# Attention with routed experts in one kernel: the reciprocal product moved between two turns, the expert slot reordered, keys copied between exponentials

## The chip, the cores and the metric

One NeuronCore of one Trainium2 chip runs the whole program. The metric is device time in microseconds (us). A core has five engines that run side by side and meet at semaphores: TensorE (PE, with its weight loads shown as PEld), VectorE (DVE), ScalarE (ACT), GpSimd (POOL) and SyncE (SP), which here only issues DMAs. Each engine takes its own instructions in the order in which the program lists them, so the place of a waiting instruction in that order is what this case is about.

## The reference, cut to what matters

```python
xn = layernorm(x)                                  # x: 16 x 512 tokens of 128
h  = rmsnorm(xn) * norm_scale
q, k, v = h @ wq * 64**-0.5, h @ wk, h @ wv        # 16 heads of 64
attn = softmax(q @ k.T) @ v @ w_out + b_out        # within each of the 16 blocks of 512
logits = silu(xn @ rw1 + rb1) @ rw2 + rb2          # router, 8 experts, the best 2
ffn = sum over the two experts e of prob_e * (silu(xn @ w1[e] + b1[e]) @ w2[e] + b2[e])
out = x + attn + ffn
```

All in float32. The experts' hidden width is 512.

## The kernel before, in words

**Ticks and units.** Each of the NB = 16 blocks of 512 tokens has 32 pieces of attention work, which are done in "ticks". There are TIMES = 256 ticks G; four of them make a unit u = G // 4 (64 units), and k = G % 4 is the tick's place in its unit. A unit is 4 head pairs (GH) by half of a block's queries; it has eight steps, two for each tick. A step s of unit u is: scores on PE (L313, into the PSUM banks 0 to 3, two at a time), the row maxima on DVE (`maxima`, L555), two exponentials on ACT with their row sums (`probs`, L911), and a turn (32x32 transposes) on DVE (`turn_probs`, L563). When all eight turns of unit u-1 are done, PE multiplies them by the values in the ticks k = 0 and k = 1 of unit u (`weighted`, L332, 128 matmuls in each), into the banks 4 to 7. DVE's `weighted` (L572, two instructions) multiplies that by the reciprocals of the row sums, which is what frees the four banks; PE's `project_out` (L345, "OP") follows in tick k = 2, and DVE adds its result into `acc` (L595 or L598).

**The reciprocals' way.** `denominators` (L581, L585) makes and turns the reciprocals at the start of tick k = 0; SP writes them to a DRAM scratch with four DMAs (`spread`, L1239), waits for these, and reads them back, spread over the partitions, as RB with two DMAs (L1244). DVE's `weighted` waits for RB.

**Keys, queries, values of the next unit.** In tick k = 2 PE makes the next unit's queries (L298, two banks), in tick k = 3 two of the next group's key tiles (L283 to L286) and two of its value tiles (L271). ACT copies them out (L890, L884, L918). The two key tiles of a tick with G % 8 = 7 are needed by the scores of the very next tick.

**The banks 4 to 7 are a ring** (`Ring`): each user takes the next bank in the order in which PE's program lists them, and waits until the bank's last user was read (`came_free`). At k = 2 the ring is aligned to bank 4.

**The second half.** Router and scatter run in the ticks below 128. From tick 139 on, the 39 expert tiles of 512 rows (NT = 39) are worked in `SLOTS`: ten at 139, 151, ... 247 (k = 3) and 29 at k = 2 of the units 35 to 63. In the slot of tile i the kernel turns the rows of tile i+1 on PE ("turn", L239 into `xg`), does the second product of tile i-1 ("y", 32 matmuls L472 into `w2`) and the first product of tile i ("h", four chunks of three matmuls, L222 to L224). ACT has, for "turn", one copy (L983) and, for each chunk of "h", a tanh (L995) and a copy with bias (L997), which frees the chunk's bank. DVE has, for "turn", the low half (L800), for "y" two instructions (`give_back`, L813 and L817), and for each chunk one `halves` (L806), which needs the chunk's L995 and L997. `LATE` puts the last two `halves` of a slot into the next tick, behind that tick's two maxima. SP fetches weights and rows at "h" of chunk 0; POOL adds the rows to the output at "back".

**Order.** `PLAN[G]` is the order written out by hand for the experts; all engines follow it. A tick's other work comes ahead of it on PE and ACT, and on DVE it stands behind the tick's turns and `project_out`. What the next tick's maxima wait for on DVE is therefore everything of the slot that DVE has in this tick.

Of the kernel before, what the change touches and what calls it, by code (L numbers as in the profile page):

```python
# [25 lines left out]
NC = HID // P  # L26
# [53 lines left out]
def block_kernel(nc, x, wq, wk, wv, wout, ns, bout, rw1, rb1, rw2, rb2, w1, w2, bias, brows, ident, tri, consts, out):  # L80
    T = x.shape[0]
    NB = T // S
# [7 lines left out]
    with ExitStack() as ctx:  # L90
# [100 lines left out]

        SLOTS = sorted([FIRST + 12 * k for k in range(NT - (UNITS - FIRST // 4 - 1))] + [4 * u + 2 for u in range(FIRST // 4 + 1, UNITS)])
        PLAN = {G: [] for G in range(TIMES + 8)}
        LATE = {G: [] for G in range(TIMES + 8)}
        PLAN[FIRST - 1].append((0, "turn"))
        for i, G in enumerate(SLOTS):
            if i + 1 < NT:
                PLAN[G].append((i + 1, "turn"))
            if i:
                PLAN[G].append((i - 1, "y"))  # L200
            PLAN[G] += [(i, "h", c) for c in range(NC)]
            LATE[G + 1] += [(i, c) for c in (2, 3)]
            if i:
                PLAN[G].append((i - 1, "back"))
        PLAN[TIMES - 1].append((NT - 1, "y"))
        PLAN[TIMES].append((NT - 1, "back"))

# [306 lines left out]
        def _(eng):  # L514
# [42 lines left out]
            def turn_probs(g, s):  # L557
                step = STEPS * g + s
                slot = place_of(g, s)[0]
                dve.wait_ge(sem["act_exp"], 2 * step + 2)  # L560
                if step >= RING:
                    dve.wait_ge(sem["pe_PV"], (step - RING) // STEPS + 1)
                dve.do.transpose(PT[:].rearrange("p c k q -> p (c k) q")[:, :, 32 * slot:32 * slot + 32],  # L563
                                 PR[:, step % PRB].rearrange("p r k -> p (r k)")).then_inc(sem["dve_tr"])
# [121 lines left out]
            def counts(r):  # L686
                dve.wait_ge(sem["dve_gate"], 15 * r + 13)
                for t in range(QT):
                    if t or r:
                        dve.wait_ge(sem["dve_pm"], 5 * r + t)  # L690
                    else:
                        dve.wait_ge(sem["dve_pm0"], 1)
                    if r >= 2:
                        dve.wait_ge(sem["pe_pos"], r - 1)
                    dve.do.tensor_tensor(PM[:, r % 2, t + 1], PM[:, r % 2, t], mask[:, t], ALU.add).then_inc(sem["dve_pm"])
                dve.wait_ge(sem["dve_pm"], 5 * r + QT)
                dve.wait_ge(sem["pe_pos"], r)
                dve.do.tensor_copy(PM[:, 1 - r % 2, 0], PM[:, r % 2, QT]).then_inc(sem["dve_pm"])
# [103 lines left out]
            def halves(i, c):  # L802
                n = i * NC + c
                dve.wait_ge(sem["act_zt"], n + 1)
                dve.wait_ge(sem["act_zz"], n + 1)
                dve.do.scalar_tensor_tensor(HH[:, i % 2, c], ZT[:, n % 2], 1.0, HH[:, i % 2, c], ALU.add, ALU.mult).then_inc(sem["dve_s"])  # L806
# [13 lines left out]
            def experts(G):  # L820
                if G == EARLY * GB + 3:
                    totals()
                for i, what, *c in PLAN[G]:
                    if what == "turn":
                        rows_low(i)
                    if what == "y":
                        give_back(i)
                    if what == "h" and c[0] < 2:
                        halves(i, c[0])

            dve.do.memset(junk[:], 0.5).then_inc(sem["dve_junk"])
# [10 lines left out]
            for G in range(TIMES + 8):  # L842
                u, k = divmod(G, 4)
                if k == 0 and 0 < u < UNITS:
                    denominators(u - 1)
                if k == 2 and 0 < u <= UNITS:
                    weighted(u - 1)
                if u < UNITS:
                    maxima(u, 2 * k)
                    maxima(u, 2 * k + 1)  # L850
                attending(G)
                between(G)
                for i, c in LATE[G]:
                    halves(i, c)
                if u < UNITS:
                    turn_probs(u, 2 * k)
                    if G % 8 == 2 and 0 < G // 8 <= NB:
                        counts(G // 8 - 1)
                    turn_probs(u, 2 * k + 1)
                route(G)  # L860
                if k == 2 and 0 < u <= UNITS:
                    project_out(u - 1)
                if G == TIMES - 1:
                    denominators(u)
                experts(G)

        @block.scalar
        def _(eng):
# [26 lines left out]
                act.do.copy(XT[:], bank[BANK["xT", r]]).then_inc(sem["act_xTs"])  # L895

            def alone(G):
                return G >= 8 * NB and G % 8 == 7 and G not in SLOTS

            def probs(g, s):  # L900
                step = STEPS * g + s
# [24 lines left out]
            def attending(G):  # L926
                b, h = divmod(G, GB)
                u, k = divmod(G, 4)
                g, first = u // 2 + 1, u % 2 * 2
                if k == 3 and g < 2 * NB:  # L930
                    if G >= 8 * NB and not alone(G):
                        keys(g, first)
                    if not alone(G):
                        keys(g, first + 1)
                    values(g, first)
                    values(g, first + 1)
                if G < 2:
                    values(0, 2 * G)
                    values(0, 2 * G + 1)
# [512 lines left out]
```

## Time and profile before

| | before |
|---|---|
| median of 3 runs | 1888.17 us (1884.29 to 1891.51) |
| the profiled execution | 1887.85 us, its span 1886.0 us |
| mean granted TensorE clock | 0.997 |
| ticks 0 to 127, a pair of units | 52.5 us |
| ticks 140 to 255, three units (with three slots at k = 2 and one at k = 3) | 96.5 us |

The page counts an engine as busy while an instruction of it runs. Matmuls are pipelined and overlap, so PE's share says little; how long a tick lasts is read from DVE's first maxima of a tick (L555) to that of the next, and its cause from the chain of waits and the timeline.

### The profile page before, as it was taken

To read this page: it belongs to the slowest core of one execution; us is meant where nothing else is said; L and a number is where in the kernel's file an instruction comes from. 1 tells how busy PE (TensorE), PEld (TensorE's weight loads), DVE (VectorE), ACT (ScalarE), POOL (GpSimd) and SP (SyncE) were. 2 spreads that over 40 slices of the span, in tenths; PEclk is the share of its full clock that TensorE was granted. 3 is DMA by queue.
4 is the path that set the end of the run, shared out by engine and by line. 5 is a ranking of instruction groups with operands and counts; after the bars stand their busy time and mean duration, and the time that the engine had idled before them with its cause. 6 is when DMAs were issued, how large, how long until landed. Compare 5 with 4: busy or idle time off the path is not lost.

```text
span 1886.0 us, 74660 instructions
## 1 busy us (share of the span) xinstructions
PE 1817.7 (96%) x32554; PEld 1177.0 (62%) x32554; DVE 1625.3 (86%) x2297; ACT 1209.1 (64%) x2987; POOL 733.0 (39%) x641
## 2 busy tenths in 40 slices
PE   8999999999999999998999999999999999999997
PEld 5555555555555555554567766767676667666765
DVE  6999999999999999989888888788888888888886
ACT  6666776666666666664666675666676666666663
POOL 4244655444544445432023334324324333333143
PEclk9999999999999999999999999999999999999999
DMA  3033321111111111111433434333433333333333
GB/s 96 22 83 109 101 95 52 42 48 37 48 37 48 48 48 46 30 40 56 110 74 78 90 73 90 78 84 78 89 74 66 92 65 87 76 84 78 79 74 56
DMA packets 154487, 130.15 MB, mean 69 GB/s; under 512 B 27664, under 2 KB 139024, under 8 KB 154128
## 3 DMA queue, kind: packets, MB, share of 16 engines
q1 hardware_dynamic: 123568, 104.65, 20.3%
q0 software_dynamic: 30592, 20.73, 8.1%
q8 instruction: 255, 4.18, 0.9%
q14 instruction: 72, 0.59, 0.1%
HBM read 93.15 MB, written 34.27 MB: 68 GB/s over the span
## 4 chain that ended last, share of the span: by engine, by line
PE 40%; ACT 28%; DVE 18%; issue 12%; DMA 1%; POOL 0%; POOLq 0%; SPq 0%; ACTq 0%; DVEq 0%
ACT PR L911 18%; PE pair L332 11%; DVE NM L555 8%; PE pair L472 8%; PE pair L313 7%; DVE PT L563 4%; PE pair L345 3%; ACT ZT L995 3%; ACT HH L997 3%; PE pair L298 3%; DVE OT L572 3%; ACT KS L884 1%; PE pair L239 1%; PE pair L388 1%; PE pair L271 1%
## 5 line engine op out<-in xcount | busy, mean ns | idle before, releaser
L911 ACT ACTIVATE PR<-pair,NM 128x512 f32<-128x512 f32 x1024 | 696.3, 697 | 536.9 <-DVE NM L555 536.4
L563 DVE STREAM_TRANSPOSE PT<-PR 128x1024 f32<-128x1024 f32 x512 | 633.2, 1241 | 119.2 <-ACT PR L911 105.7
L555 DVE TENSOR_REDUCE NM<-pair 128x2 f32<-128x1024 f32 x512 | 598.0, 1208 | 19.6 <-PE pair L313 18.9
L313 PE MATMUL pair<-KS,QS 64*32 64x512 f32 x8192 | 505.3, 598 | 16.6 <-ACT PR L911 9.3
L332 PE MATMUL pair<-PT,V 32*64 32x256 f32 x16384 | 479.7, 378 | 17.9 <-ACT HH L997 9.7
L332 PEld LDWEIGHTS pair<-PT,V 32*64 32x64 f32 x16384 | 383.6, 131 | 166.6 <-issue 107.3
L1174 POOL DMA_INDIRECT out<-YS,IDW x156 | 248.4, 1592 | 536.8 <-DVE YS L817 334.3
L313 PEld LDWEIGHTS pair<-KS,QS 64*32 64x32 f32 x8192 | 122.7, 106 | 261.7 <-issue 157.4
L911 ACT ACTIVATION_READ_ACCUMULATOR PR<-pair,NM 128x1 f32 x1024 | 218.9, 214 | 0.0
L995 ACT ACTIVATE ZT<-pair,BT 128x512 f32<-128x512 f32 x156 | 109.8, 704 | 108.1 <-PE pair L224 108.0
L1132 POOL DMA_INDIRECT slots<-XR,IDX x128 | 124.4, 972 | 73.9 <-issue 38.5
L472 PE MATMUL pair<-E,HH 128*128 128x128 f32 x1248 | 148.1, 277 | 2.9 <-DVE HH L806 2.9
L472 PEld LDWEIGHTS pair<-E,HH 128*128 128x128 f32 x1248 | 144.1, 194 | 4.4 <-DVE HH L806 3.8
L806 DVE SCALAR_TENSOR_TENSOR HH<-ZT,HH 128x512 f32<-128x512 f32 x156 | 104.1, 688 | 43.6 <-ACT HH L997 43.6
L298 PE MATMUL pair<-HF,WQ 128*128 128x256 f32 x512 | 126.1, 389 | 10.1 <-DVE OT L572 9.3
L298 PEld LDWEIGHTS pair<-HF,WQ 128*128 128x128 f32 x512 | 92.1, 190 | 62.2 <-DVE OT L572 49.5
L1121 POOL TENSOR_TENSOR TH<-TH,HS 128x512 f32<-128x512 f32 x64 | 82.1, 1282 | 120.1 <-ACT HS L951 120.1
L345 PE MATMUL pair<-OT,WO 128*128 128x256 f32 x512 | 123.6, 384 | 2.2 <-DVE OT L572 2.2
L271 PE MATMUL pair<-WV,HF 128*32 128x128 f32 x4096 | 125.1, 274 | 0.0
L271 PEld LDWEIGHTS pair<-WV,HF 128*32 128x32 f32 x4096 | 107.8, 110 | 23.4 <-issue 23.3
L345 PEld LDWEIGHTS pair<-OT,WO 128*128 128x128 f32 x512 | 94.7, 190 | 37.7 <-issue 9.5
L997 ACT ACTIVATE HH<-pair,BT 128x512 f32<-128x512 f32 x156 | 110.4, 708 | 0.0
(129 smaller groups left out, 1798.1 us busy)
## 6 DMA issues: line engine op xcount, KB each, us to landing
RB<-l_rows SPq DMA_DIRECT2D x128, 256.0 KB, 4.3
E<-w_tab SPq DMA_DIRECT2D x39, 512.0 KB
XG<-slots SPq DMA_DIRECT2D x39, 264.0 KB, 4.0
E<-in_w SPq DMA_DIRECT2D x39, 256.0 KB, 3.9
xin<-in_x SPq DMA_DIRECT2D x16, 256.0 KB, 2.8
XQ<-in_x SPq DMA_DIRECT2D x16, 256.0 KB, 3.1
l_rows<-RT SPq DMA_DIRECT2D x256, 2.0 KB
w_tab<-SPL SPq DMA_DIRECT2D x8, 512.0 KB, 2.6
```

Source lines behind the costliest of these rows:

```text
L271: m = pe.do.matmul(bank[bk][32 * a:32 * a + 32, j * P:j * P + P], HF[:, keys], WV[:, pair], start=True, stop=True, tile_position=(0, 32 * a))
L298: m = pe.do.matmul(bank[bk][:, 256 * i:256 * i + 256], WQ[:, pair], HF[:, 256 * half:256 * half + 256], start=True, stop=True)
L313: m = pe.do.matmul(bank[2 * (s % 2) + r][32 * c:32 * c + 32, :], QS[rows, u % 2, c, at:at + 32], KS[rows, g % 2, c, :], start=True, stop=T ...
L332: m = pe.do.matmul(bank[GH + a][DH * c:DH * c + DH, 0:256], V4[rows, g % 2, k, DH * c:DH * c + DH], moving, start=(k == 0), stop=(k == 15) ...
L345: m = pe.do.matmul(bank[bk][:, 0:256], WO[:, GH * (u // 2 % 2) + a, :], OT[:, a, :], start=(a == 0), stop=(a == GH - 1))
L472: m = pe.do.matmul(bank[bk][:, t * P:(t + 1) * P], HH[:, i % 2, c, t * P:(t + 1) * P], E2[:, i % 2, c * P:(c + 1) * P], start=(c == 0), st ...
L555: dve.do.tensor_reduce(NM[:, step % 4], pairs[s % 2][:], AX.X, ALU.max, negate=True).then_inc(sem["dve_max"])
L563: dve.do.transpose(PT[:].rearrange("p c k q -> p (c k) q")[:, :, 32 * slot:32 * slot + 32], PR[:, step % PRB].rearrange("p r k -> p (r k)" ...
L911: act.do.activation(PR[:, step % PRB, r, :], bank[2 * (s % 2) + r], ACT.Exp, bias=NM[:, step % 4, r:r + 1], accum_out=RS[:, g % 2, r, at:a ...
L995: act.do.activation(ZT[:, n % 2], ps, ACT.Tanh, bias=BT[:, i % 3, 8 + c:9 + c], scale=0.5).then_inc(sem["act_zt"])
L997: act.do.activation(HH[:, i % 2, c], ps, ACT.Identity, bias=BT[:, i % 3, c:c + 1]).then_inc(sem["act_zz"])
L1174: pool.do.indirect_dma_start(out, bass.IndirectOffsetOnAxis(ap=IDW[:, i % 4, t, 0:1].bitcast(U32), axis=0), YS[:, i % 2, t, :], None, comp ...
```

## The change

Three edits. (1) DVE's `weighted(u-1)` moves from the head of tick k = 2, ahead of the maxima, to tick k = 1, between its two turns. (2) In `PLAN` the four chunks "h" of a slot come first, then "turn", then "y"; all four `halves` are in the slot's own tick, and `LATE` is gone. (3) `alone(G)` now holds in the first half too: in the ticks with G % 8 = 7 below 128 ACT copies both key tiles between the exponentials of the tick's two steps, instead of one between and one behind. In the second half it stays as it was.

```diff
         PLAN = {G: [] for G in range(TIMES + 8)}
-        LATE = {G: [] for G in range(TIMES + 8)}
         PLAN[FIRST - 1].append((0, "turn"))
         for i, G in enumerate(SLOTS):
+            PLAN[G] += [(i, "h", c) for c in range(NC)]
             if i + 1 < NT:
                 PLAN[G].append((i + 1, "turn"))
             if i:
-                PLAN[G].append((i - 1, "y"))
-            PLAN[G] += [(i, "h", c) for c in range(NC)]
-            LATE[G + 1] += [(i, c) for c in (2, 3)]
-            if i:
-                PLAN[G].append((i - 1, "back"))
+                PLAN[G] += [(i - 1, "y"), (i - 1, "back")]
...
-                    if what == "h" and c[0] < 2:
+                    if what == "h":
                         halves(i, c[0])
...
-                if k == 2 and 0 < u <= UNITS:
+                if k == 2 and u == UNITS:
                     weighted(u - 1)
...
-                for i, c in LATE[G]:
-                    halves(i, c)
                 if u < UNITS:
                     turn_probs(u, 2 * k)
                     if G % 8 == 2 and 0 < G // 8 <= NB:
                         counts(G // 8 - 1)
+                    if k == 1 and u:
+                        weighted(u - 1)
                     turn_probs(u, 2 * k + 1)
...
             def alone(G):
-                return G >= 8 * NB and G % 8 == 7 and G not in SLOTS
+                return G % 8 == 7 and G not in SLOTS
...
-                    if G >= 8 * NB and not alone(G):
+                    if G in SLOTS or G % 8 == 3 and G >= 8 * NB:
                         keys(g, first)
```

## Rows read from the trace of the kernel before

**Rows 1.** The page: busy us, share of the span, instructions.

```profile
PE 1817.7 (96%) x32554; PEld 1177.0 (62%) x32554; DVE 1625.3 (86%) x2297; ACT 1209.1 (64%) x2987; POOL 733.0 (39%) x641
```

**Rows 2.** Who waited for whom, whole span: us in total, times, longest.

```profile
ACT PR L911 <- DVE NM L555: 536.4, 214, 6.1
ACT ZT L995 <- PE pair L224: 108.0, 38, 3.7
```

**Rows 3.** Timeline, slot at k = 2: start, duration, engine, line, [idle before].

```profile
1590.67 2.34 DVE L555 TENSOR_REDUCE NM<-pair 128x2 f32<-128x1024 f32 x2
...
1592.17 1.89 PE L345 MATMUL pair<-OT,WO 128*128 128x256 f32 x8
...
1594.33 3.74 PE L472 MATMUL pair<-E,HH 128*128 128x128 f32 x32
...
1595.70 1.25 DVE L563 STREAM_TRANSPOSE PT<-PR 128x1024 f32<-128x1024 f32 x1 [1.07 <-ACT PR L911]
...
1596.87 0.39 DVE L598 TENSOR_TENSOR acc<-pair,acc 128x256 f32<-128x256 f32 x1
...
1598.11 0.69 DVE L813 SCALAR_TENSOR_TENSOR YS<-pair,B 128x512 f32<-128x512 f32 x1 [0.25 <-PE pair L472]
...
1598.80 0.69 ACT L995 ACTIVATE ZT<-pair,BT 128x512 f32<-128x512 f32 x1 [2.65 <-PE pair L224]
1598.83 0.69 DVE L817 TENSOR_TENSOR YS<-YS,IDW 128x512 f32<-128x512 f32 x1
...
1599.96 0.69 ACT L995 ACTIVATE ZT<-pair,BT 128x512 f32<-128x512 f32 x1
```

**Rows 4.** Timeline, DVE alone: that slot's end, then the slot at k = 3.

```profile
1601.97 2.36 DVE L555 TENSOR_REDUCE NM<-pair 128x2 f32<-128x1024 f32 x2
...
1605.45 2.37 DVE L563 STREAM_TRANSPOSE PT<-PR 128x1024 f32<-128x1024 f32 x2
...
1611.17 0.69 DVE L813 SCALAR_TENSOR_TENSOR YS<-pair,B 128x512 f32<-128x512 f32 x1 [1.80 <-PE pair L472]
...
1615.42 1.18 DVE L555 TENSOR_REDUCE NM<-pair 128x2 f32<-128x1024 f32 x1
```

**Rows 5.** Timeline, ACT alone, the slot at k = 3.

```profile
1606.97 1.18 ACT L918 COPY V<-pair 128x512 f32<-128x512 f32 x2
```

**Rows 6.** Timeline, DVE alone, the slot at k = 2 two units on.

```profile
1657.17 2.34 DVE L555 TENSOR_REDUCE NM<-pair 128x2 f32<-128x1024 f32 x2
...
1668.78 2.36 DVE L555 TENSOR_REDUCE NM<-pair 128x2 f32<-128x1024 f32 x2
```

**Rows 7.** Timeline, DVE alone, first half: an even unit's tick k = 1.

```profile
388.93 2.58 DVE L563 STREAM_TRANSPOSE PT<-PR 128x1024 f32<-128x1024 f32 x2
```

**Rows 8.** Timeline, DVE alone, first half: an odd unit's ticks k = 1 and k = 3.

```profile
413.38 2.36 DVE L555 TENSOR_REDUCE NM<-pair 128x2 f32<-128x1024 f32 x2 [0.53 <-PE pair L313]
...
416.12 2.59 DVE L563 STREAM_TRANSPOSE PT<-PR 128x1024 f32<-128x1024 f32 x2
...
430.87 1.25 DVE L563 STREAM_TRANSPOSE PT<-PR 128x1024 f32<-128x1024 f32 x1 [0.58 <-ACT PR L911]
```

**Rows 9.** Timeline, PE and ACT, first half: second half of the weighted values, the second key copy.

```profile
386.14 3.71 PE L332 MATMUL pair<-PT,V 32*64 32x256 f32 x128
...
414.06 3.71 PE L332 MATMUL pair<-PT,V 32*64 32x256 f32 x128
...
430.71 0.60 ACT L884 COPY KS<-pair 128x512 f32<-128x512 f32 x1
```

**Rows 10.** Timeline, SP's reads of RB in two units, and DVE's product in the first.

```profile
1164.64 1.25 SPq L1244 DMA_DIRECT2D RB<-l_rows  x2
...
1171.42 1.29 DVE L572 TENSOR_TENSOR OT<-pair,RB 128x512 f32<-128x512 f32 x2 [0.71 <-DMA RB<-l_rows]
...
1581.93 1.25 SPq L1244 DMA_DIRECT2D RB<-l_rows  x2
```

**Rows 11.** All reads of RB (L1244): time from issue to landing.

```profile
DMA to landing us min/median/max: 3.5/4.3/5.7
```

## The prediction

> **What bounds the kernel now.** I read the page first, then the waits, then the timeline of all engines over one repetition in each half. The page [rows 1] names no bound: PE has always something in flight, DVE is busy for 86%, ACT for 64%. The waits [rows 2] show where to look: ACT waits 536 us for maxima from DVE and, in 38 of the 39 expert slots, 108 us in all for the first product on PE. The second of these is what edit 2 takes up. But an idle ACT costs nothing unless ACT is what ends last, so each edit has to be followed to the next maxima.
>
> In the timeline the bound changes hands within each unit. In the first half, PE is late from an even unit's tick k = 2 to the maxima of the next odd unit's tick k = 1, which wait 0.53 us for its scores [rows 8]; from there on DVE, with ACT's exponentials between its maxima and its turns, is late until the next even unit's tick k = 2. In a k = 2 slot, PE's row of work (output projection, turn, second product, first product) ends with ACT's first tanh, and ACT's four chunks then end last [rows 3].
>
> **Edit 2, slots at k = 2.** Let T be the start of the tick's first maxima, 1590.67 in rows 3; the next tick's stand at T+11.30 in rows 4. A later slot has 1668.78-1657.17 = 11.61 [rows 6]. I take 11.45, their middle, for each of the 28 such slots ahead of the last.
>
> After the change PE starts the first product at the projection's end, T+3.4 (1592.17+1.89) [rows 3], and ACT can begin its tanh when the last exponential is done, some 4.9 after T (the turn that waits for it starts at 1595.70, T+5.0 [rows 3]; the copy L983 that stands there now comes last). So ACT's wait of 2.65 [rows 3] is gone. What is late next follows from two orders.
>
> First the ring. A k = 2 tick takes its banks from bank 4 on: queries, (a turn of h or of acc in half of the blocks' ticks,) the projection OP, and then the slot's. The fourth chunk of "h" is now always four places behind OP and so gets its bank; it must wait for DVE's sum into acc. Before, the second product or a turn stood between, and the fourth chunk came long after. The sum ends at 1596.87+0.39 = T+6.6, behind the turn that waits 1.07 for the exponentials, at which nothing is changed [rows 3]. PE then has, one after the other: three matmuls 0.70 (rows 3: the first tanh at 1598.80 follows the second product's end and one such chunk), turn 0.43, second product 3.74 [rows 3]. That ends at T+6.65+0.70+0.43+3.74 = T+11.5.
>
> Second DVE's order. The two `give_back` now stand behind all four `halves` and ahead of the next maxima. Start to start they take 0.72 (1598.83-1598.11) and the second 0.69 [rows 3]: T+11.55+0.72+0.69 = T+12.95 for the next maxima. ACT's side is earlier: chunks of 1.16 (1599.96-1598.80) [rows 3] from T+4.9 end at T+9.5, its copy at T+10.2, the last `halves` at T+10.3, the low half at T+10.9.
> So the tick grows from 11.45 to 12.95, **+1.5; 28 slots: +42 us**. With no wait for the sum the second product would end 0.6 earlier, and this would be +0.9, or +25.
>
> **What gives some of it back.** In the tick behind a slot the two late `halves` are gone and the four turns and maxima run as in a tick without slot.
> - Slot at k = 3 (10). Before 1615.42-1601.97 = 13.45 [rows 4], and the following ticks k = 0 and 1 12.6 together, as in a timeline of the next unit. After, from the first maxima M: exponentials until M+3.95, four copies of keys and values at M+6.0 (1606.97 and 1.18 are the last two of them) [rows 5], and only then the four chunks, whose banks these copies free: chunk 1 free at M+8.2, second product until M+12.0, the two give-backs, reciprocals 0.4: M+13.8, +0.35. Then 5.2 and 6.55 for the two ticks, with the product waiting 0.3 for PE: -0.85. Together **-5 us** for ten.
> - Plain k = 3 tick behind a slot, G % 8 = 3 (10): -0.5, but the copies of the values end later against DVE, so the weighted values of the next unit begin 0.35 later and edit 1 waits for them: -0.5+0.5, **0 us**.
> - G % 8 = 7, not in a slot (9): -0.2 and, in edit 1, -0.2: **-3 us**.
> - The last unit and the tail: the last slot +2, all `halves` earlier, so the last second product no longer waits: **-1 us**.
>
> **Edit 1 in the first half.** The work only changes place on DVE; what changes is what it waits for. In even units the turn ends at 388.93+1.25 = 390.2, PE's weighted values at 386.14+3.71 = 389.85 [rows 7, 9]: no wait, and the 0.1 between the two turns is covered; -0.18 for 15 units, -2.7. In odd units the turn ends at 416.12+1.25 = 417.4 but PE at 414.06+3.71 = 417.8 [rows 8, 9]: the product starts there, 0.36 later than the second turn did: 15 units (two with 0.7), +6.1. PE itself gains a little where its queries had waited for the product, but it then waits for ACT's queries as before: nothing.
>
> The product now is 1.2 us earlier (one turn) and so nearer to RB's landing. SP issues the reads between 2.8 (1581.93, a unit begun at 1579.08) and 4.4 (1164.64, one begun at 1160.21) after the unit's first maxima, in others up to 4.9, and the second is landed some 5.2 after the first's issue (0.6 to 0.9 for its own issue, 4.3 median) [rows 10, 11]. DVE is ready at 9.15 (even) or 10.2 (odd units of the first half). With 5.2 on every unit's issue, ten of the fifteen even first-half units wait 0.1 to 0.85, in sum +6.8 (with the covered 0.1), and the second half +5.5. Bounds: 0, if all land as the earliest, at 7.5; 63 x 1.4 = +88, if all land as the latest, 11.2 in rows 10, where the product waited even in its old place. I take **+12 us**, since 5.2 is the middle of what the landings show.
> The Trainium skill (DMA: Bandwidth & Descriptors, section "Anatomy of one DMA — SWDGE (gpsimd) path") gives a DMA about 2.0 us fixed plus its bytes by 436 GB/s; as an estimate from that page, write and read back would be done some 5 to 6 after the maxima and the product would never wait, which takes these 12 us off. The landings of rows 11, 3.5 at the least, speak against it here.
>
> **Edit 3.** In the 16 ticks with G % 8 = 7 of the first half the second key copy (0.60, 0.58 start to start) [rows 9] goes ahead of the second step's exponentials, whose turn on DVE already waits 0.58 for them [rows 8]. DVE has nothing else to do there and is late from there to the next unit's k = 2. PE's scores, which now wait for the copy, come earlier, but the maxima behind them are held by DVE. **16 x 0.58 = +9.3 us.** Bounds 0 (if PE's earlier scores paid it back) and 9.3; DVE's rows from 430.87 on run without a gap, so I take the upper.
>
> **Sum** on the profiled execution: 42-5-3-1 (slots), -2.7+6.1+9.3 (first half), +12 (RB) = +57.7; 1887.85+57.7 = **1945 us**. That execution is within 0.4 us of the median, so no correction.
>
> **Rivals.**
> - *ACT was the bound of the slots (faster).* If the next maxima could be made while ACT does its chunks, all of the 108 us [rows 2] would go: 1887.85-108+24 = about 1805. It decides at one point: whether the second product ends before T+9. For it: the chain of before passes through PE's second product and ACT's chunks in every slot. Against: three chunks, OP's bank and the turn stand ahead of the second product now, and it alone takes 3.74. Chance 0.05.
> - *The sum isn't waited for long, and the second key copy costs nothing (slower by less).* The slots +25 in place of +42, edit 3 nothing: 1945-17-9 = 1919. Against: bank and order are fixed in the program. Chance 0.13.
> - *RB is late every time (slower by more).* Half way to the bound of +88: 1945+38 = 1983. For it: latencies of L1244 up to 5.7 and issues of up to 4.9. Chance 0.06.
> - *Nothing to be seen*: gains in the ticks behind the slots equal the losses. It would take 1.5 us more gain behind each slot than the late `halves` (1.3 us of DVE) can give. Chance 0.03.
> - *Forecast*: 1945, own range 1928 to 1964, chance 0.73.
>
> **Numbers.** The range takes in the forecast's and reaches to the smaller loss: 1920 to 1968. About 0.5% (9 us) is what a measurement of this kernel can tell from no change. Faster 0.05, same 0.03, slower 0.92.
>
> **What would show each step.** In the profile after: first maxima to first maxima of a k = 2 slot 12.9 (before 11.3 to 11.6), PE idle about 1 us ahead of the fourth chunk until acc, and DVE's L813 counterpart waiting for the second product; ACT's wait for the first product from 108 to under 20 us, its wait for maxima larger by about as much. In the first half: the product waiting for PE in odd units, for RB in some even ones; a wait of 1.15 in place of 0.58 ahead of the last turn of the G % 8 = 7 ticks. A k = 2 slot of under 12.3 would make the bank's step wrong; one under 11.4 the whole forecast.

## The result, and the profile after

The changed kernel took 1962.12 us (median of four runs, 1958.83 to 1963.69), the kernel before 1889.25 us beside it: ratio 1.0387, with a 95% interval of 1.0362 to 1.0413, so slower. The profiled execution took 1962.82 us, its span is 1961.0 us, 75.0 more than before, at a mean granted clock of 0.994. The prediction said 1945 us with a range of 1920 to 1968: sign and mechanism came out, the size was 17 us short.

The page of the kernel after (busy us, share of the span, instructions), to be laid beside rows 1:

```profile
PE 1838.1 (94%) x32554; PEld 1180.0 (60%) x32554; DVE 1640.9 (84%) x2297; ACT 1210.3 (62%) x2987; POOL 734.4 (37%) x641
```

The work on DVE and ACT is what it was, within 1%, and its shares fell: nearly all of the 75 us are idle time. Where they stand is told by the waits. The waits of the kernel after, whole span (who waited for whom, us in total, times, longest), to be laid beside rows 2. The edit moved every line number: L551 here was L555, L907 was L911, L568 was L572, L309, L328 and L468 were L313, L332 and L472.

```profile
ACT PR L907 <- DVE NM L551: 715.9, 253, 6.1
...
PE pair L218 <- DVE acc L594: 23.9, 15, 2.2
...
DVE OT L568 <- PE pair L328: 22.6, 30, 8.4
...
PE pair L218 <- DVE acc L591: 16.2, 14, 1.5
...
DVE OT L568 <- DMA RB<-l_rows: 15.6, 21, 1.9
```

ACT's 108.0 us for the first product [rows 2] are gone, and its wait for the maxima grew by 179.5 us: ACT now waits in one place for longer than it did in two. Three waits are new or have grown. PE's matmul of the first product (L218) waits for DVE's sum into acc in 29 slots, 40 us in all. DVE's product waits for PE in 30 units where it did in one, the last, and for RB in 21 units where it did in one (rows 10).

The slot itself. Timeline of the kernel after, all engines, a slot at k = 2 (start, duration, engine, line, [idle before]); rows 3 and 4 show the same of before:

```profile
1685.80 2.31 DVE L551 TENSOR_REDUCE NM<-pair 128x2 f32<-128x1024 f32 x2
...
1690.64 0.72 ACT L991 ACTIVATE ZT<-pair,BT 128x512 f32<-128x512 f32 x1
...
1690.82 1.25 DVE L559 STREAM_TRANSPOSE PT<-PR 128x1024 f32<-128x1024 f32 x1 [1.07 <-ACT PR L907]
...
1691.98 0.39 DVE L594 TENSOR_TENSOR acc<-pair,acc 128x256 f32<-128x256 f32 x1
...
1692.43 0.50 PE L218 MATMUL pair<-X,E 128*128 128x512 f32 x1 [0.96 <-DVE acc L594]
...
1693.66 3.74 PE L468 MATMUL pair<-E,HH 128*128 128x128 f32 x32
...
1697.44 0.69 DVE L809 SCALAR_TENSOR_TENSOR YS<-pair,B 128x512 f32<-128x512 f32 x1 [0.56 <-PE pair L468]
1698.16 0.69 DVE L813 TENSOR_TENSOR YS<-YS,IDW 128x512 f32<-128x512 f32 x1
1698.77 2.35 DVE L551 TENSOR_REDUCE NM<-pair 128x2 f32<-128x1024 f32 x2
```

Maxima to maxima: 1698.77-1685.80 = 12.97, against 11.30 and 11.61 before [rows 3, 4, 6]; the prediction said 12.95. Read from the end: the maxima follow the second give-back without a gap, the first give-back waited 0.56 for the second product, this one stands behind the fourth chunk of the first product, and that waited 0.96 for the sum, which stands behind the turn that waits 1.07 for the exponentials. (0.96 is the shortest of these waits; the 29 have 1.38 in the mean and 2.23 at most. Their start varies, their end is the sum's.) ACT starts its first tanh at T+4.84, where rows 3 have T+8.13, and nothing is gained by these 3.3 us.

The first half. Timeline of the kernel after, DVE alone, an odd unit's tick k = 1 (first two rows) and k = 3; rows 8 show the same of before:

```profile
426.52 1.25 DVE L559 STREAM_TRANSPOSE PT<-PR 128x1024 f32<-128x1024 f32 x1
...
428.27 1.29 DVE L568 TENSOR_TENSOR OT<-pair,RB 128x512 f32<-128x512 f32 x2 [0.51 <-PE pair L328]
...
442.16 1.25 DVE L559 STREAM_TRANSPOSE PT<-PR 128x1024 f32<-128x1024 f32 x1 [1.07 <-ACT PR L907]
```

The product stands between the turns and waits 0.51 for PE; the last turn of the G % 8 = 7 tick waits 1.07 in place of 0.58. Both were to be seen by the prediction, at 0.36 and at 1.15.

**The ledger.** First maxima to first maxima of every tick, after less before, on the two profiled executions:

| where | predicted | measured | ticks, after and before |
|---|---|---|---|
| 28 slots at k = 2 | +42 | +43.5 | mean 13.08 and 11.5 |
| 10 slots at k = 3 and the two ticks behind | -5 | +1.3 | 14.05 and 13.44 typical |
| plain G % 8 = 3 ticks and the two behind | 0 | +4.0 | -5.2, +1.8, +7.4 |
| G % 8 = 7 outside slots and the two behind | -3 | +0.4 | -1.8, 0, +2.2 |
| the product's waits for RB, second half | +5.5 | in the three rows above | 10.3 in 12 waits |
| last slot and tail | -1 | +4.1 | slot 13.17 and 9.60, tail +0.6 |
| first half, odd units, k = 1 | +6.1 | +7.9 | 6.86 and 6.42 typical |
| first half, even units, k = 1, with RB's waits | +4.1 | +7.7 | 6.19 to 8.51 |
| first half, keys | +9.3 | +7.6 | 7.81 and 7.32 |
| everything else before tick 136 | 0 | -1.6 | |
| sum | 58 | 75 | |

### The profile page after: what moved, and what is told of

Its sections match the earlier page's. It is cut to its first block, busy times and chain, and to the rows that moved or that the text cites. A ratio compares the mean times of both kernels' runs of the same rounds, so it can differ in the third digit from the quotient of the medians.

```text
span 1961.0 us, 74661 instructions
## 1 busy us (share of the span) xinstructions
PE 1838.1 (94%) x32554; PEld 1180.0 (60%) x32554; DVE 1640.9 (84%) x2297; ACT 1210.3 (62%) x2987; POOL 734.4 (37%) x641
## 4 chain that ended last, share of the span: by engine, by line
PE 32%; DVE 24%; ACT 22%; issue 9%; DMA 9%; SPq 2%; POOL 0%; POOLq 0%; ACTq 0%; DVEq 0%
ACT PR L907 14%; PE pair L328 13%; DVE NM L551 8%; PE pair L468 7%; DVE PT L559 7%; PE pair L309 6%; DMA RB<-l_rows 5%; DVE OT L568 4%; DMA l_rows<-RT 3%; ACT QS L886 3%; ACT KS L880 2%; SPq L1235 2%; PE pair L384 1%; ACT ZT L991 1%; DVE YS L809 1%
## 5 line engine op out<-in xcount | busy, mean ns | idle before, releaser
L907 ACT ACTIVATE PR<-pair,NM 128x512 f32<-128x512 f32 x1024 | 694.3, 690 | 716.1 <-DVE NM L551 715.9
L551 DVE TENSOR_REDUCE NM<-pair 128x2 f32<-128x1024 f32 x512 | 596.3, 1205 | 15.2 <-PE pair L309 14.0
L309 PE MATMUL pair<-KS,QS 64*32 64x512 f32 x8192 | 511.7, 600 | 21.0 <-ACT PR L907 18.3
L328 PE MATMUL pair<-PT,V 32*64 32x256 f32 x16384 | 479.0, 379 | 14.6 <-ACT XT L891 3.1
L328 PEld LDWEIGHTS pair<-PT,V 32*64 32x64 f32 x16384 | 386.7, 132 | 160.7 <-issue 85.9
L309 PEld LDWEIGHTS pair<-KS,QS 64*32 64x32 f32 x8192 | 119.7, 106 | 265.2 <-ACT PR L907 130.8
L907 ACT ACTIVATION_READ_ACCUMULATOR PR<-pair,NM 128x1 f32 x1024 | 211.4, 206 | 0.0
L802 DVE SCALAR_TENSOR_TENSOR HH<-ZT,HH 128x512 f32<-128x512 f32 x156 | 111.8, 718 | 69.8 <-ACT HH L993 68.8
L468 PE MATMUL pair<-E,HH 128*128 128x128 f32 x1248 | 149.7, 279 | 2.9 <-ACT HH L993 2.9
L468 PEld LDWEIGHTS pair<-E,HH 128*128 128x128 f32 x1248 | 145.5, 195 | 6.3 <-DVE HH L802 3.7
L218 PE MATMUL pair<-X,E 128*128 128x512 f32 x156 | 70.2, 450 | 51.4 <-DVE acc L594 23.9
```

Of the source, the lines that this page charges most:

```text
L309: m = pe.do.matmul(bank[2 * (s % 2) + r][32 * c:32 * c + 32, :], QS[rows, u % 2, c, at:at + 32], KS[rows, g % 2, c, :], start=True, stop=T ...
L328: m = pe.do.matmul(bank[GH + a][DH * c:DH * c + DH, 0:256], V4[rows, g % 2, k, DH * c:DH * c + DH], moving, start=(k == 0), stop=(k == 15) ...
L468: m = pe.do.matmul(bank[bk][:, t * P:(t + 1) * P], HH[:, i % 2, c, t * P:(t + 1) * P], E2[:, i % 2, c * P:(c + 1) * P], start=(c == 0), st ...
L551: dve.do.tensor_reduce(NM[:, step % 4], pairs[s % 2][:], AX.X, ALU.max, negate=True).then_inc(sem["dve_max"])
L907: act.do.activation(PR[:, step % PRB, r, :], bank[2 * (s % 2) + r], ACT.Exp, bias=NM[:, step % 4, r:r + 1], accum_out=RS[:, g % 2, r, at:a ...
```

## The experiments

The kernels ran in three groups, each on a chip of its own. In the second group the kernel before took 1888.09 us, as at first; in the first it took 2042.39 and in the third 2029.53. A ratio is therefore read only against the runs of its own group; what the traces show of the first and third group's chips comes with the first experiments. "Ticks" are always first maxima to first maxima.

### Each edit alone (first and third group)

e1_product and e1_again make edit 1 alone:

```diff
-                if k == 2 and 0 < u <= UNITS:
+                if k == 2 and u == UNITS:
                     weighted(u - 1)
...
+                    if k == 1 and u:
+                        weighted(u - 1)
                     turn_probs(u, 2 * k + 1)
```

e2_slot and e2_again make edit 2 alone:

```diff
+            PLAN[G] += [(i, "h", c) for c in range(NC)]
             if i + 1 < NT:
                 PLAN[G].append((i + 1, "turn"))
...
-            PLAN[G] += [(i, "h", c) for c in range(NC)]
-            LATE[G + 1] += [(i, c) for c in (2, 3)]
...
-                    if what == "h" and c[0] < 2:
+                    if what == "h":
                         halves(i, c[0])
```

e3_keys and e3_again make edit 3 alone:

```diff
-                return G >= 8 * NB and G % 8 == 7 and G not in SLOTS
+                return G % 8 == 7 and G not in SLOTS
...
-                    if G >= 8 * NB and not alone(G):
+                    if G in SLOTS or G % 8 == 3 and G >= 8 * NB:
                         keys(g, first)
```

e1_product:

> Edit 1 alone on the kernel before: the product with the reciprocals moved between the turns of tick k = 1, the slots and the key copies as before. Theory (the parts add up, and each is a wait on DVE): +20 to +26 us over before (ratio 1.011 to 1.014); odd units' tick k = 1 of the first half 6.86 in place of 6.42 us (the product waits for PE's weighted values), even ones 6.2 where RB is in time and up to 7.6 where it is late. Rival (RB is late only because the reordered slots move the weights' and rows' transfers onto it): within 6 us of before, even units of the first half 6.2 throughout.

e1_again:

> Edit 1 alone on the kernel before, once more, on whichever chip comes. Theory, from the ticks of the runs so far: on a chip without the late instructions +13 to +20 us (ratio 1.007 to 1.011), nearly all of it in the first half, since the old order's slots are bound by PE and take back in tick k = 2 what tick k = 1 loses; the slots at k = 2 about 0.4 shorter. Rival (edit 1 costs the same in both halves): +25 to +33 us.

e2_slot:

> Edit 2 alone on the kernel before: the slot's chunks first, then the turn, then the second product, all four halves in the slot's tick. Theory: the k = 2 slots last 12.95 us in place of 11.5, the k = 3 slots 0.6 more, their following tick 1.0 less, plain k = 3 ticks 0.2 to 0.5 less: +35 to +43 us over before (ratio 1.019 to 1.023). Rival (the slots' order costs only together with the moved product, whose later maxima push the sum into acc back): under +20 us.

e2_again:

> Edit 2 alone on the kernel before, once more. Theory: +33 to +42 us (ratio 1.0175 to 1.022), all of it from tick 139 on; edits 1 and 2 together then cost 10 to 15 us more than their sum, because the slots no longer take back what the product's waits cost. Rival (the parts add up): +52 us, what is left of after's 77 when 17 and 8 are taken off.

e3_keys:

> Edit 3 alone on the kernel before: both key copies between the exponentials in the ticks with G % 8 = 7 below 128. Theory: each such tick 0.5 us longer (7.8 for 7.3), because DVE's last turn waits for exponentials that stand behind one more copy: +7 to +9 us (ratio 1.004 to 1.005). Rival (PE's scores, released 0.5 us earlier by the copy, pay it back): 0, the following tick k = 0 shorter by 0.5.

e3_again:

> Edit 3 alone on the kernel before, once more. Theory: 0.45 to 0.5 us in each of the 16 ticks with G % 8 = 7 below 128, +7 to +8 us (ratio 1.0035 to 1.0045) on a chip without the late instructions; there, as in the first group, nothing. Rival (PE's earlier scores pay it back): within 2 us of before on every chip.

| edit alone | first group | third group |
|---|---|---|
| 1, the product | 2053.13, ratio 1.0045 [1.0029, 1.006] | 2043.99, 1.0073 [1.0057, 1.0088] |
| 2, the slot | 2077.34, 1.0173 [1.0157, 1.0189] | 2065.45, 1.0169 [1.0153, 1.0184] |
| 3, the keys | 2043.27, 1.0006 [0.9995, 1.0017] | 2035.19, 1.0024 [1.0015, 1.0034] |

Edit 2 carries most of the loss, +35 and +36 us. Its slots at k = 2 have 13.00 us in both, as in the whole change. Edit 1 adds 11 and 14 us, edit 3 adds 1 (its interval takes in 0) and 6 (its interval does not). Of the forecasts, e1_product's (+20 to +26) and e3_keys' (+7 to +9) were missed, and e3_again's, that nothing would be seen on such a chip. In sum these are 47 and 56 us, where the first chip showed 73 for the whole; so either the parts don't add, or these chips hide some of it. The first question went to the second group; on the second the trace of e3_again has something to say. Timeline of e3_again, PE alone, then DVE alone ("<-issue": the engine waited for nothing that the profile shows), in one tick with G % 8 = 7 of the first half:

```profile
483.88 0.45 PE L271 MATMUL pair<-WV,HF 128*32 128x128 f32 x4 [0.28 <-issue]
...
486.83 0.42 PE L239 MATMUL pair<-idn,XR 128*128 128x128 f32 x1 [0.66 <-issue]
...
489.68 5.37 PE L313 MATMUL pair<-KS,QS 64*32 64x512 f32 x31 [0.37 <-issue]
```

```profile
484.43 1.25 DVE L563 STREAM_TRANSPOSE PT<-PR 128x1024 f32<-128x1024 f32 x1 [1.06 <-ACT PR L911]
...
494.25 2.36 DVE L555 TENSOR_REDUCE NM<-pair 128x2 f32<-128x1024 f32 x2 [6.97 <-PE pair L313]
```

PE stops for "issue" again and again, its scores come late, and the maxima wait 6.97 us for them: that tick has 15 us where the kernel before had 7.32 in its profiled execution. Its granted clock, 1.00 until 486, is 0.50 from 488 to 492. 13 of the 16 such ticks of the first half are so (12.3 to 15.7 us), 13 in every other trace of the first and third groups too, and none in those of the second group. Where a tick waits 7 us for PE anyway, half a microsecond of a key copy is hidden. So what edit 3 costs was hidden in those ticks, as I read it, and only the three ticks without such a lateness show it: 7.81 in both e3_again and the kernel after, against 7.32. Three times 0.49 is 1.5 us: that fits the first group's 1, and leaves 4 of the third group's 6 unexplained. The edit's price depends on this cover, and its ratios here don't bear on 1888 us. The same trace shows a second cover: edit 3 touches no slot, and yet the 29 slots at k = 2 have 11.82 us in the mean (11.90 in e3_keys), where the kernel before had 11.46. Of edit 2's 1.54 us for each slot 0.36, 10.5 us in all, would be hidden there.

For edit 1, the waits of e1_product in its own trace:

```profile
DVE OT L572 <- PE pair L332: 38.0, 51, 8.5
...
DVE OT L572 <- DMA RB<-l_rows: 9.1, 11, 1.9
```

The product waits for RB in 11 units though the slots are the old ones, so the rival, that only the reordered slots make RB late, is refuted. On this chip it waits for PE in 51 units, in 14 of the even ones of the first half too, where the kernel after has no such wait.

e1_again and e3_again differ, on one chip, in edit 1 and edit 3. In the second half e1_again's ticks k = 1 are 15.8 us longer in sum, and its slots at k = 2 are 13.9 us shorter. In the old order, then, most of what the product loses in tick k = 1 is given back in the slot behind it.

### The whole again, the order alone, the halves alone, the product without RB (second group)

a0_after is the changed kernel once more.

> The kernel after once more, unchanged, beside the kernels of this group. On a chip where PE gets its instructions as in the profile shown ahead of the prediction: ratio 1.036 to 1.041. On the chip of the first group, where PE is late with instructions in the ticks with G % 8 = 7 of the first half: edit 3 and part of edit 1 lie under that, ratio 1.024 to 1.030.

It took 1965.7 us against 1888.09, ratio 1.0413 [1.0395, 1.043]: +77.6, with the slots at k = 2 at 13.02 in the mean. The result repeats.

```diff
 e6_order_only: the new order on PE and ACT, LATE kept
+            PLAN[G] += [(i, "h", c) for c in range(NC)]
             if i + 1 < NT:
                 PLAN[G].append((i + 1, "turn"))
             if i:
                 PLAN[G].append((i - 1, "y"))
-            PLAN[G] += [(i, "h", c) for c in range(NC)]
             LATE[G + 1] += [(i, c) for c in (2, 3)]
```

> The kernel before with the new order of a slot (chunks, turn, second product) but the last two halves still in the next tick. Theory (the order on PE and DVE sets the tick: second product, two give-backs, next maxima): slots at k = 2 12.95 us as in after, and the ticks behind them keep their late halves (6.1 and 6.2): +45 to +53 us over before, more than the whole of edit 2 costs. Rival (the halves in the slot's own tick are what holds the next maxima): slots at k = 2 near 11.5, under +10 us.

1936.18 us, ratio 1.0248 [1.0231, 1.0266]: +48. Timeline of e6_order_only, DVE alone, a slot at k = 2:

```profile
1664.71 2.34 DVE L555 TENSOR_REDUCE NM<-pair 128x2 f32<-128x1024 f32 x2
...
1676.36 0.69 DVE L813 SCALAR_TENSOR_TENSOR YS<-pair,B 128x512 f32<-128x512 f32 x1 [0.76 <-PE pair L472]
...
1677.70 2.35 DVE L555 TENSOR_REDUCE NM<-pair 128x2 f32<-128x1024 f32 x2
```

12.99, as with the whole change, though two `halves` (1.3 us of DVE) are not in this tick: DVE only waits longer for the second product, 0.76 in place of 0.56. So the order costs the slot its 1.5 us, not the moved `halves`. In the new order these in fact pay: a plain G % 8 = 3 tick behind a slot has 6.15 here and 5.62 in the whole change, the tick behind a slot at k = 3 has 5.72 and 5.20.

```diff
 e5_halves_only: the old order, all halves in the slot's own tick
-            LATE[G + 1] += [(i, c) for c in (2, 3)]
...
-                    if what == "h" and c[0] < 2:
+                    if what == "h":
                         halves(i, c[0])
```

> The kernel before with the old order of a slot but all four halves in its own tick. Theory: there ACT's fourth chunk ends last, 12.9 us after the first maxima, and the last halves and the next maxima stand behind it: slots at k = 2 13.5 us, those at k = 3 15.7, the ticks behind them 0.5 and 1.0 shorter: +60 to +72 us. Rival (the halves are short and DVE has time): under +20 us.

1968.86 us, ratio 1.0433 [1.0413, 1.0453]: +81, more than the +60 to +72 expected. Timeline of e5_halves_only, all engines, a slot at k = 2:

```profile
1689.25 2.35 DVE L553 TENSOR_REDUCE NM<-pair 128x2 f32<-128x1024 f32 x2
...
1697.25 0.69 ACT L991 ACTIVATE ZT<-pair,BT 128x512 f32<-128x512 f32 x1 [2.52 <-PE pair L222]
...
1702.09 0.69 DVE L804 SCALAR_TENSOR_TENSOR HH<-ZT,HH 128x512 f32<-128x512 f32 x1 [0.46 <-ACT HH L993]
1702.70 2.35 DVE L553 TENSOR_REDUCE NM<-pair 128x2 f32<-128x1024 f32 x2
```

In the old order ACT's chunks come last, and a `halves` in the slot's tick puts the next maxima behind ACT's fourth chunk: 13.45 here, 13.68 in the mean, and 16.49 in the slots at k = 3, 0.8 above what I had expected. Neither half of edit 2 gains by itself, and both together are no gain: the order takes the wait away from ACT and gives it to DVE, behind the second product.

e4_product_no_rb is edit 1 with a constant tile in RB's place, so that DVE can't wait for RB. It leaves out the reciprocals, so the attention's values are unscaled; SP still writes and reads them:

```diff
-                dve.wait_ge(*side("RB", g, 32))
...
-                    dve.do.tensor_tensor(OT[:, a:a + 2, :], pairs[2 + a // 2][:, :, 0:256], RB[:, a:a + 2, :],
+                    dve.do.tensor_tensor(OT[:, a:a + 2, :], pairs[2 + a // 2][:, :, 0:256], RK[:],
```

> Edit 1 alone, and the product takes a constant tile in place of RB, so it waits for no transfer; SP still writes and reads the reciprocals. What is left out: the reciprocals of the row sums, so the attention's values are unscaled. Theory (what edit 1 costs is half PE's weighted values, half RB's landing): tick k = 1 of even units of the first half 6.2 us throughout, of odd ones 6.86 as with edit 1; 8 to 14 us less than edit 1 alone. Rival (RB's landing costs nothing, the late units are something else): as edit 1 alone, with the same late ones.

1888.22 us, ratio 1.0003 [0.9993, 1.0012]: no difference. Its waits, then DVE alone in a slot at k = 2:

```profile
DVE OT L574 <- PE pair L333: 26.0, 38, 7.2
```

```profile
1588.57 1.29 DVE L574 TENSOR_TENSOR OT<-pair,RK 128x512 f32<-128x512 f32 x2 [0.40 <-PE pair L333]
...
1590.94 2.32 DVE L556 TENSOR_REDUCE NM<-pair 128x2 f32<-128x1024 f32 x2
...
1601.96 2.36 DVE L556 TENSOR_REDUCE NM<-pair 128x2 f32<-128x1024 f32 x2
```

Three things follow. First, the 15 even units of the first half that have a product take 6.19 in tick k = 1 (before 6.39 in the mean), odd ones 6.86 (before 6.42): the covered 0.2 is as predicted, the wait for PE nearly so. Second, their sum over the even units is 10.6 us below that of a0_after: that is what the real RB costs there, GpSimd's part (below) included. Third, in the second half the ticks k = 1 cost +5.4 and the slots give back 9.4: the slot above has 11.02 where rows 3 and 4 have 11.30. My reading is that PE's row of work sets the end of an old slot, so a later first maxima only shortens the tick, and that in the new order the slot's end hangs on ACT's exponentials and DVE's sum, which follow the first maxima: the slots have 13.00 without edit 1 (e2_slot, e2_again, e6_order_only) and 13.02 with it (a0_after), so nothing is given back.

### The sum into acc between the two turns (first group)

```diff
 a1_sum_early: the changed kernel and
+                    if k == 2 and G in SLOTS:
+                        project_out(u - 1)
                     turn_probs(u, 2 * k + 1)
...
-                if k == 2 and 0 < u <= UNITS:
+                if k == 2 and 0 < u <= UNITS and G not in SLOTS:
                     project_out(u - 1)
```

> The kernel after, with one thing more: in the slots at k = 2 DVE adds the projection into acc between the tick's two turns, where it waits 1.07 us for exponentials anyway, so that the bank of the fourth chunk is free 2.2 us earlier. Theory (the fourth chunk waits for that bank, and the second product behind it ends last): the slots at k = 2 fall from 12.96 to 12.3 us, 28 x 0.6 = 17 us less than after, ratio to before 1.028 to 1.031. Rival (what ends last is ACT's four chunks and DVE's work behind them, not PE): no change against after, 1.038.

2091.19 us, ratio 1.0239 [1.0223, 1.0254]. Most of the slots have 12.62 against 12.96 to 13.04 in the kernel after: 0.34 to 0.42 gained, not the 0.65 expected. Every fourth has 13.14 as in the kernel after, so nothing. The kernel after did not run on this chip, so the gain is read from the slots alone. Timeline of a1_sum_early, all engines, a slot at k = 2:

```profile
1813.22 2.32 DVE L551 TENSOR_REDUCE NM<-pair 128x2 f32<-128x1024 f32 x2
...
1817.10 0.39 DVE L594 TENSOR_TENSOR acc<-pair,acc 128x256 f32<-128x256 f32 x1
...
1819.51 0.63 PE L235 MATMUL pair<-idn,XG 128*128 128x128 f32 x4 [0.32 <-ACT HH L995]
...
1820.67 3.81 PE L468 MATMUL pair<-E,HH 128*128 128x128 f32 x32 [0.53 <-ACT HH L995]
...
1825.85 1.22 DVE L551 TENSOR_REDUCE NM<-pair 128x2 f32<-128x1024 f32 x1
```

The sum is done at T+4.3 (before T+6.6), PE no longer waits for it, and 12.63 from maxima to maxima are left: now the turn and the second product wait for the banks of the first chunks, which ACT's second function (L995) frees. So the bank wait was real, and the next ones in the ring lay some 0.3 us behind it. The +0.9 for each slot that the prediction gave for no wait for the sum would have needed all of them away.

### GpSimd held back (third group)

```diff
 a3_pool_gate: the changed kernel and, ahead of GpSimd's attention_rows
+                    if b:
+                        pool.wait_ge(sem["dve_tr"], 2 * G + (2 if G >= 8 * NB else 1))
```

> The kernel after, with GpSimd's two tensor operations for the next block's rows held back until the turns of the tick in which the program has them (they ran up to two ticks early, beside DVE's halves). Theory (a DVE instruction with two operands in SBUF stands still while such a GpSimd operation runs): the two slots of 15.15 us fall to 14.05, the halves of 2.0 and 1.5 us are gone, 3 to 6 us less than after. Rival (those halves are slow for another reason): the two slots stay at 15.1.

Two of the changed kernel's slots at k = 3 have 15.15 us where the others have 14.05. In these the `halves` run longer than 0.69 while GpSimd has a tensor operation. Timeline of the kernel after, DVE alone, then POOL alone; DVE's first row and POOL's first two are from the first half:

```profile
236.06 2.65 DVE L669 SCALAR_TENSOR_TENSOR gt<-gt,CON 128x32 f32<-128x32 f32 x1
...
1258.97 4.20 DVE L802 SCALAR_TENSOR_TENSOR HH<-ZT,HH 128x512 f32<-128x512 f32 x3 [1.94 <-ACT HH L993]
```

```profile
236.37 1.29 POOL L1155 TENSOR_TENSOR SPL<-RAW,SPL 128x512 fp32r<-128x512 f32 x1
237.60 1.05 POOL L1061 TENSOR_TENSOR HR<-xin,mv 128x512 f32<-128x512 f32 x1
...
1258.83 1.62 POOL L1061 TENSOR_TENSOR HR<-xin,mv 128x512 f32<-128x512 f32 x1
...
1260.53 1.38 POOL L1064 TENSOR_TENSOR HR<-HR,sqo 128x512 f32<-128x512 f32 x1
```

L669 is 0.17 us elsewhere; three `halves` take 4.20 in place of 2.07. With GpSimd made to wait for the turns of the tick in which the program has these operations (in the first half for its first turn), DVE of a3_pool_gate in the same slot:

```profile
1372.08 2.35 DVE L551 TENSOR_REDUCE NM<-pair 128x2 f32<-128x1024 f32 x2
...
1379.32 0.69 DVE L802 SCALAR_TENSOR_TENSOR HH<-ZT,HH 128x512 f32<-128x512 f32 x1 [1.93 <-ACT ZT L991]
...
1386.11 1.18 DVE L551 TENSOR_REDUCE NM<-pair 128x2 f32<-128x1024 f32 x1
```

14.03 in place of 15.16, each `halves` at 0.69. The kernel took 2091.4 us against 2029.53, ratio 1.0304 [1.0288, 1.032]. The changed kernel without the gate did not run on that chip, so what the gate is worth in the whole time isn't measured. By the traces it is at most the time by which DVE's two-input instructions exceed their usual length: 10.5 us in the changed kernel, 0.25 with the gate, 2.6 in the kernel before. Part of this stands beside other waits. The same 62 us lie 6 above the sum of the three edits alone on that chip.

## Why the prediction was right in sign and 17 us short

**Right.** The views of rows 3 and 4 carried the largest term to within 1.5 us: the bank of the fourth chunk, the sum behind the turn, three matmuls, the turn, the second product, two give-backs, 12.95 against 12.96 to 13.14 in 27 of the 28. The 28th, with 14.61, had a lower clock (last section), which is 1.6 of the term's 43.5. e6_order_only shows that the order is the cause, a1_sum_early that the bank is a link in it. The rival in which ACT is the bound is refuted in every slot: ACT begins 3.3 us earlier and the tick is longer. That nothing would be seen, and that RB would be late every time, are refuted too: 21 of the units waited.

**The step that failed most: what comes behind a slot.** "After, from the first maxima M ... +0.35" and "-0.85" for the two ticks behind gave -5 for ten; +1.3 was measured. The ticks behind came out as said (-10.2 and +1.4, so -0.88 each). The slot at k = 3 did not: 14.05 in place of 13.8, two of them with GpSimd's 1.1 more, and the first, at tick 139, which has no second product, grew from 9.92 to 12.33. I had worked out one typical slot and multiplied by ten. That the slots missed their +0.35 by 0.26 each in the usual case is a part of it that no run explains.

**The last slot.** "The last slot +2 ... -1 us" was +4.1. The +2 was right for the order: e2_slot, e2_again, e6_order_only and a3_pool_gate have 11.55 to 11.58 where the kernel before has 9.60. The kernel after and a0_after have 13.17, because there the second product ran at a lower clock and took 5.1 us in place of 3.7 (last section). The gain in the tail isn't there either (+0.6 in place of -3). The last second product no longer waits 2.86 for `halves`, and PE's weighted values begin 3.5 us nearer to the tick's maxima, as foreseen. But DVE's last operation then waits 4.01 for the reading back of `out`, which SP issues behind GpSimd's last write of expert rows; before it waited 1.09. I had not followed that path.

**Waits of the product.** In the first half the wait for PE was sized 0.36 and made the odd units' ticks 0.44 longer: 7.9 in place of 6.1, in 17 ticks and not 15, the last of them, behind tick 128, with 0.89. RB's landings were sized at 12 us, 6.8 in the first half and 5.5 in the second; the waits are 5.3 in 9 units and 10.3 in 12 units. So the middle of the landings was a fair choice for the sum, and too low for the second half. The figure of the Trainium skill (DMA: Bandwidth & Descriptors, "Anatomy of one DMA — SWDGE (gpsimd) path") is given there for DMAs that GpSimd issues. I had put it on DMAs that SP issues; the estimate made so, by which the product would never wait, is refuted by these 21 waits, and the page's own case is not tested here. What the sum left out is the product's wait for PE in the second half: from tick 136 on 12.7 us in 12 waits, of which 7.2 stood in the kernel before. Both waits together make the ticks k = 1 of the second half longer by 7.4, 2.2 and 1.4 us. I had let edit 1 pay for itself behind the plain G % 8 = 3 ticks ("-0.5+0.5"), where +4.0 was measured (-5.2 in the ticks themselves, +9.2 in the two behind). e4_product_no_rb and e1_again show that in the old order the slot gives such time back; edit 2 takes that away.

**Keys.** +7.6 in place of +9.3: 0.49 for 15 of the 16 ticks (0.23 for the last), not 0.58. The copy's 0.58 stand start to start, but the turn behind waits 1.07 in place of 0.58, which is 0.49. I had taken the operation's length where the growth of the wait was due.

**Even units.** +7.7 in place of +4.1: the covered 0.19 is there (6.19 where nothing disturbs, 6.38 before), the rest is RB and two units (8.51 and 7.97) in which GpSimd held DVE.

**Why the parts sum to less.** In the third group they sum to 56 us, and the whole took 77.6 in the second. Two pieces of these 21 us have a measure: 10.5 us by which the old slots are longer on that chip, and what the old slots give back to edit 1, 13.9 us in e1_again and 9.4 in e4_product_no_rb. They cover the difference, but each comes from one pair of traces, and the second belongs to any chip: a3_pool_gate, the whole change less up to 10.5 us of GpSimd's, is 6 above the parts on that same chip, which would put the whole 6 to 16 above them. The split is worked out, not tested: the whole change did not run on that chip, nor edit 2 alone on the second group's.

What stays open is why PE stops for "issue" in 13 of 16 ticks on two chips, and why the clock fell in two slots of the kernel after.

## What to carry to other kernels

When a wait is removed by putting work earlier in one engine's order, follow the row of every other engine to the point that the next stage waits for: here ACT's wait went, and the second product, 3.7 us on PE, came to stand last instead. An edit that costs little in a stage where another engine ends last can cost its full price as soon as a second edit makes that stage end elsewhere, so two edits are not priced apart. Work out the first and the last member of a repeated pattern on their own.

## What the runs showed of the hardware

**DVE beside GpSimd.** DVE's instructions with two SBUF inputs were held up while GpSimd's tensor operations ran: 0.17 became 2.65 us beside operations of 1.29 and 1.05, 0.69 became 1.5 and 2.0 beside 1.62 and 1.38, and with GpSimd kept away they were at 0.69. I had not looked for it. How much of it a kernel has depends on how its schedule falls: 2.6 us before, 6.0 in e2_again, 10.5 after. The Trainium skill (SBUF — State Buffer, "Who interferes with whom") says that a DVE instruction with two SBUF inputs contends with a GpSimd instruction that reads SBUF; these rows agree. They don't show which of the two gives way: the record of L669 begins 0.31 us ahead of GpSimd's first operation, and still it ends with GpSimd's second.

**A lower clock in two slots.** One slot at k = 2 has 14.61 us, and the last one 13.17. Timeline of the kernel after, PE alone, in these two slots, and then the windows view of the first (the stretch and its length; busy us and instructions of PE, PEld, DVE, ACT and POOL; mean granted clock; DMA share; GB/s):

```profile
1243.73 0.51 PE L218 MATMUL pair<-X,E 128*128 128x512 f32 x1 [1.77 <-DVE acc L594]
...
1245.22 5.13 PE L468 MATMUL pair<-E,HH 128*128 128x128 f32 x32
...
1926.86 0.50 PE L218 MATMUL pair<-X,E 128*128 128x512 f32 x1 [2.23 <-DVE acc L594]
...
1927.87 5.13 PE L468 MATMUL pair<-E,HH 128*128 128x128 f32 x32
```

```profile
1244.00:1251.00 7.00, 7.00 (x55) 6.30 (x62) 3.56 (x6) 3.26 (x6) 0.00 (x0) 0.76 0.19 52
```

The same last slot in a3_pool_gate, PE alone:

```profile
2052.74 0.50 PE L218 MATMUL pair<-X,E 128*128 128x512 f32 x1 [2.23 <-DVE acc L594]
...
2053.55 3.73 PE L468 MATMUL pair<-E,HH 128*128 128x128 f32 x32
```

In the kernel after both second products took 5.13 in place of 3.74, at a granted clock of 0.72 in the mean: part of the stretch ran at 1.2 GHz, the rest at 2.4. In the first slot this is 1.4 of the 1.6 us that it has above its like, in the last 1.4 of 1.6 above a3_pool_gate's 11.55. PE had waited for the sum just before, but the wait alone doesn't decide: in the same trace four other slots waited 1.74 to 1.77 for the sum and kept 3.74 at a clock of 1.00; in a0_after no slot but the last fell; and a3_pool_gate waited 2.23 in its last slot and kept 3.73. What else it takes is not shown here.

**The same kernel on other chips.** The kernel before took 1888 us in the first runs and in the second group, 2030 and 2042 us on the chips of the other two. e3_again's profiled execution is 145 us longer than that of the kernel before, of which 95 lie in the first half's ticks with G % 8 = 7, in 13 of which PE stops for "issue", and 34 in the ticks k = 0 up to tick 128. Over the first half its mean granted clock is 0.957, and 1.000 in the kernel before. Whether the clock fell because PE stopped or for a reason of its own, these traces don't separate, and no experiment here says why PE stops.
